# Attention: PE issues the next unit's first group of scores ahead of the router's rank matmuls and the V projection

## The chip, the cores and the metric

The kernel runs as one program on one core of one Trainium2 chip. The metric is the device time in microseconds of that core, from start to end of the program; smaller is better. The engines are PE (matrix multiplications), DVE (vector work), ACT (activation functions), POOL (general work, here also indirect DMAs) and SP (it only issues DMAs). Each has its own list of instructions, and they wait for each other through semaphores.

## The reference

The input is 64 sequences of 64 tokens with 128 channels and a context of the same shape. Four gated blocks follow each other: cross-attention, a top-2 mixture of 8 experts, a second kind of cross-attention, and a second mixture.

```python
x = x + tanh(g_xattn[0]) * L0_xattn(layernorm(x), ctx, ctx)
x = x + tanh(g_ffn[0])   * L0_ffn(layernorm(x))     # router, top 2 of 8 experts
x = x + tanh(g_xattn[1]) * L1_xattn(layernorm(x), ctx)
x = x + tanh(g_ffn[1])   * L1_ffn(layernorm(x))
```

The change lies in the first block. There, with 16 heads of 8 channels:

```python
wq = (q @ wq_w.T + wq_b).reshape(b, t, H, DH)
wk = (k @ wk_w.T + wk_b).reshape(b, t, H, DH)
wv = (v @ wv_w.T + wv_b).reshape(b, t, H, DH)
scores = einsum('bthd,bshd->bhts', wq, wk) / sqrt(DH)
probs = softmax(scores, axis=-1)
attn = einsum('bhts,bshd->bthd', probs, wv).reshape(b, t, d)
return attn @ wo_w.T + wo_b
```

The router of the second block (the logits, the two best experts, and where in the list of its expert each token goes) is worked out on the side, in the same loop as the attention.

## The kernel before

The tokens are 32 chunks of 128. A **unit** is two chunks (256 tokens, four sequences), and attention has 16 of them (`UA`). Each engine runs its own copy of a software pipeline, `it_a(u, s)`, whose order within a turn is written out by hand; turns go from -3 to 15, those from 3 to 10 in a hardware loop of two turns a pass. PE's turn `u` works on several units at once, one line of the code for each:

- `a_s(u + 1, g)`: scores of the next unit, four groups g of four heads, on `QT` and `Kb` (both are parts of the tensor `QK`), into bank 0 or 1 (L1572). Its first group waits for `a_qks`.
- `a_pt(u, g)`: transposes of the exponentials `Pr` of this unit (L1542). `a_pv(u, g)`: their product with V (L1590).
- `a_v(u)`: the V projection of this unit into bank 5 (L1555). It waits for `a_nrm`, since bank 5 holds the attention result of unit u - 1 until DVE has read it.
- `a_xt(u + 2)`, `a_qk(u + 2)`: transposes of the normalised tokens `xn` and the Q and K projections (L1562, L1563) of the unit after the next.
- `a_at(u - 1)`, `a_y(u - 1)`: the output projection of the unit before.
- `r_x(u - 2)`, `r_lg(u - 2)`, `r_rank(u - 3)`: the router. `r_rank` is five small bf16 matmuls (L1626 to L1630) on `chosen`; they count which place in its expert's list each token gets.

DVE's turn begins with `r_pos(u - 3)` (tile `pos`, L954), which waits for the ranks, then small router work up to `rowu` (L969), then the layer norm of unit u + 3 (tile `xn`, L838) and of the router's unit (tile `xr`), then `a_vs(u)` (tile `Vb`, L852), which copies V out of bank 5, and then for each group of unit u + 1 `a_max` (tile `mx`, L860) and `a_sub` (tile `Pr`, L864), which read the scores. It ends with the router's choice (`chosen`, L946), `a_rec` (L869) and `a_nrm` (tile `att`, L874).

ACT's turn copies PE's transposes out (`a_pts`, L590), takes the exponentials of `Pr` (L584), and between the second and the third of these scales and masks the Q and K of unit u + 2 in `a_qks` (four of L576 and four of L578), on which the first group of scores of that unit, in the next turn, depends.

POOL sends each router unit's tokens to their experts' lists with four indirect DMAs (L439) after `rowu`, and works out `pe`, a term of the weights (L432), which DVE's `den` (L922) needs. SP loads `cT`, the context of unit u + 2, once `a_v(u)` is done (L374).

Of the kernel before, what the change touches and what calls it, by code (L numbers as in the profile page):

```python
# [97 lines left out]
def flamingo(nc, x, ctx_tok, ctx_t, wq, wk, wv, wo, cols, rows, gates, consts, far,  # L98
             f0_wg, f0_w12, f0_w3, wqv, f1_wg, f1_w1, f1_w2, out):
    with ExitStack() as stack:  # L100
# [160 lines left out]
        def S(name):  # L261
            if name not in names:
                names[name] = sem(name)
            return names[name]
# [37 lines left out]
        def has(u, units=UA):  # L302

            return not isinstance(u, int) or 0 <= u < units
# [12 lines left out]
        def wait(eng, semaphore, value):  # L317

            if not isinstance(value, int) or value > 0:
                eng.wait_ge(semaphore, value)  # L320
# [1211 lines left out]
        def _(pe):  # L1532
# [7 lines left out]
            def transposes(done, dst, src, n):  # L1540
                for c in range(n):
                    last = nc.tensor.transpose(dst[:, P * c:P * (c + 1)], src(c), ident)  # L1542
                last.then_inc(S(done), 1)


            def a_xt(u, s):
                pe.wait_ge(S("a_ln"), u + 1)
                wait(pe, S("a_qks"), u)
                transposes("a_xt", bank[4], lambda c: xn[:, s, c, :], 2)

            def a_v(u, s):
                pe.wait_ge(S("a_nrm"), 1 + u)
                for b in range(4):
                    for e in range(2):
                        last = mm(bank[5][L * e:L * (e + 1), P * b:P * (b + 1)], cT[:, s, L * b:L * (b + 1)],  # L1555
                                  wv_eo[:, e, :], start=True, stop=True)
                last.then_inc(S("a_v"), 1)

            def a_qk(u, s):
                pe.wait_ge(S("a_xts"), u + 1)  # L1560
                pe.wait_ge(ld_cT[s], (u - s) * 8 + 16)
                mm(bank[4][:, 0:2 * P], wq_s[:], xT[:, 0, 0:2 * P], start=True, stop=True)  # L1562
                mm(bank[4][:, 2 * P:4 * P], wk_s[:], cT[:, s, 0:2 * P], start=True, stop=True).then_inc(S("a_qk"), 1)  # L1563

            def a_s(u, s, g):
                if g == 0:
                    pe.wait_ge(S("a_qks"), u + 1)
                wait(pe, S("a_sub"), u * 4 + (g - 1))
                for p in range(2):
                    for b in range(2):  # L1570
                        t = P * p + L * b
                        last = mm(bank[g % 2][L * b:L * (b + 1), 256 * p:256 * (p + 1)], QT[:, s, g, t:t + L],  # L1572
                                  Kb[:, s, :, t:t + L], start=True, stop=True)
                last.then_inc(S("a_s"), 1)

            def a_pt(u, s, g):
                pe.wait_ge(S("a_exp"), u * 4 + (g + 1))
                wait(pe, S("a_pts"), u * 4 + g)
                transposes("a_pt", bank[6 + g % 2], lambda c: Pr[:, s, g, P * c:P * (c + 1)], 4)

            def a_pv(u, s, g):
                pe.wait_ge(S("a_pts"), 1 + u * 4 + (g + 1))
                if g == 0:
                    pe.wait_ge(S("a_vs"), u + 1)
                for p in range(2):
                    for h in range(2):
                        for b in range(2):
                            m = (p * 8 + 2 * g + h) * 18
                            c = P * (2 * p + h) + L * b
                            last = mm(bank[5][L * b:L * (b + 1), m:m + 18], PT[:, g, c:c + L],  # L1590
                                      Vb[:, s, 2 * p + b, 2 * g + h, :], start=True, stop=True)
                if g == NG - 1:
                    last.then_inc(S("a_pv"), 1)

            def a_at(u):
                pe.wait_ge(S("a_nrm"), 1 + u + 1)
                pe.wait_ge(S("a_x"), 1 + u)
                transposes("a_at", bank[2], lambda c: att[:, D * c:D * (c + 1)], 2)

            def a_y(u):  # L1600
                pe.wait_ge(S("a_ats"), u + 1)
                mm(bank[2][:, 2 * P:4 * P], onb[:], rbias[:, 0:1, :].to_broadcast([P, 2, D]), start=True, stop=False, skip_group_check=True)
                for c in range(2):
                    last = mm(bank[2][:, P * (2 + c):P * (3 + c)], attT[:, P * c:P * (c + 1)], wo_s[:],
                              start=False, stop=True, skip_group_check=True)
                last.then_inc(S("a_y"), 1)
# [4 lines left out]
            def r_x(w, s):  # L1611
                pe.wait_ge(S("r_ln"), w + 1)
                pe.wait_ge(S("r_run"), w + 1)
                transposes("r_xt", bank[3], lambda c: xr[:, s, c, :], 2)

            def r_lg(w):
                pe.wait_ge(S("r_xts"), w + 1)
                for c in range(2):
                    last = mm(bank[3][:, 2 * P + E * c:2 * P + E * (c + 1)], xT[:, 1, P * c:P * (c + 1)], f0g_s[:], start=True, stop=True)
                last.then_inc(S("lgp"), 1)  # L1620

            def r_rank(w):

                pe.wait_ge(S("r_m"), w + 1)
                of = [bank[3][:, RK + E * c:RK + E * (c + 1)] for c in range(3)]
                mm(of[0], upb[:], chosen[:, 0, :], start=True, stop=True)  # L1626
                mm(of[1], onb[:], chosen[:, 0, :], start=True, stop=False)
                mm(of[1], upb[:], chosen[:, 1, :], start=False, stop=True)
                mm(of[2], onb[:], chosen[:, 0, :], start=True, stop=False)
                mm(of[2], onb[:], chosen[:, 1, :], start=False, stop=True).then_inc(S("r_rank"), 1)  # L1630

            def t_row(h):

                n = NW if h == 0 else NB - NW
                pe.wait_ge(S("t_col"), h + 1)
                mm(bank[3][0:1, TB:TB + NBH], first_row[:, h:h + 1], cst[:, C_ID + h * NBH:C_ID + (h + 1) * NBH], start=True, stop=True)
                for k in range(2):
                    w = C_BD + k * NB + h * NW
                    last = mm(bank[3][0:1, TB + NBH + n * k:TB + NBH + n * (k + 1)], en[:, h:h + 1], cst[:, w:w + n], start=True, stop=True)
                last.then_inc(S("t_row"), 1)  # L1640
# [4 lines left out]
            def it_a(u, s):  # L1645
                if has(u):
                    a_pt(u, s, 0)
                    a_pt(u, s, 1)
                if isinstance(u, int) and u == UT + 1:
                    pe.wait_ge(S("table"), 1)  # L1650
                if has(u - 3):
                    r_rank(u - 3)
                if has(u):
                    a_v(u, s)
                if has(u + 1):
                    a_s(u + 1, 1 - s, 0)
                if has(u - 1):
                    a_at(u - 1)
                if has(u + 2):
                    a_xt(u + 2, s)  # L1660
                if has(u + 1):
                    a_s(u + 1, 1 - s, 1)
                if has(u - 2):
                    r_x(u - 2, s)
                if has(u):
                    a_pt(u, s, 2)
                if has(u + 1):
                    a_s(u + 1, 1 - s, 2)
                if has(u + 2):
                    a_qk(u + 2, s)  # L1670
                if has(u):
                    a_pt(u, s, 3)
                if has(u - 1):
                    a_y(u - 1)
                if has(u - 2):
                    r_lg(u - 2)
                if has(u + 1):
                    a_s(u + 1, 1 - s, 3)
                if has(u):
                    a_pv(u, s, 0)  # L1680
                    a_pv(u, s, 1)
                    a_pv(u, s, 2)
                    a_pv(u, s, 3)
                if isinstance(u, int) and u == UT:
                    pe.wait_ge(S("lgs"), u - 1)
                    t_row(0)

            pipelined(pe, it_a, -3, 3, UT, UA)


# [312 lines left out]
```

## Time and profile before

| | us |
|---|---|
| median of 3 runs | 578.22 |
| lowest, highest | 575.12, 578.43 |
| the profiled execution's own time | 575.86 |
| its span, first to last instruction | 574.2 |
| PE busy, DVE busy, ACT busy, POOL busy | 503.0, 415.4, 316.8, 234.2 |

The rows of the next section come from that one profiled execution; their times count from the start of its span. 1.7 us of its time lie outside the span. The attention pipeline takes the part from about 20 to 232 us, and the steady turns with the router in them begin at about 67 us. Of the whole chain of work that ended last, 48% is PE, 20% DVE, 16% time in which the engine waited for nothing that the profile shows, 8% POOL and 4% ACT.

### The profile page before, as it was taken

What the parts mean: (1) busy time and instruction counts of PE and PEld (TensorE: products, weight loads), DVE (VectorE), ACT (ScalarE), POOL (GpSimd) and SP (SyncE); (2) the same over time, 40 slices, a digit from 0 to 9 for tenths busy, and PEclk for the clock granted to TensorE, in tenths of its full rate; (3) what the DMA queues carried; (4) which work ended last, traced back from release to release, by engine and by line L of the source; (5) the groups of instructions that cost most, each with busy time, mean ns of one, the idle gap of its engine ahead of it and who ended that gap; (6) DMA issues with size and microseconds to landing.
All of it is one profiled execution on the core that took longest, in us unless ns stands there. A gap on an engine that the chain in (4) does not pass through costs nothing.

```text
span 574.2 us, 14728 instructions
## 1 busy us (share of the span) xinstructions
PE 503.0 (88%) x4438; PEld 407.4 (71%) x4439; DVE 415.4 (72%) x1690; ACT 316.8 (55%) x777; POOL 234.2 (41%) x328
## 2 busy tenths in 40 slices
PE   0599999999988989878999999987989987997997
PEld 0267776777767667666778777866879975877897
DVE  4687888898989788556765567663777995575883
ACT  1378866677777764344555554554553555443453
POOL 2510255554454645445000545520566763022330
PEclk9999999999999999889999999996997999798999
DMA  8503011100000211135554334320010112000011
GB/s 246 241 10 85 23 36 33 32 27 27 27 27 29 67 47 32 48 107 170 163 165 121 107 107 110 93 66 15 23 28 12 50 43 61 6 1 0 2 39 37
DMA packets 48126, 36.80 MB, mean 64 GB/s; under 512 B 6466, under 2 KB 43970, under 8 KB 47812
## 3 DMA queue, kind: packets, MB, share of 16 engines
q1 hardware_dynamic: 31332, 21.13, 12.2%
q0 software_dynamic: 4640, 9.45, 5.7%
q10 hardware_dynamic: 12096, 5.51, 3.4%
q8 instruction: 28, 0.46, 0.4%
q14 instruction: 30, 0.25, 0.1%
HBM read 22.44 MB, written 13.63 MB: 63 GB/s over the span
## 4 chain that ended last, share of the span: by engine, by line
PE 48%; DVE 20%; issue 16%; POOL 8%; ACT 4%; another core or an unknown queue 2%; POOLq 1%; DVEq 1%; DMA 0%
PE bank L1542 10%; PE bank L1739 6%; PE bank L1837 5%; PE bank L1723 4%; POOL sent L439 4%; PE bank L1917 3%; PE bank L1725 3%; PE bank L1724 3%; PE bank L1572 3%; PE bank L1825 2%; DVE xn L838 2%; DVE mx L860 1%; DVE hgg L1415 1%; PE bank L1814 1%
## 5 line engine op out<-in xcount | busy, mean ns | idle before, releaser
L455 POOL DMA_INDIRECT yg<-done,gidx x64 | 63.8, 997 | 54.7 <-PE bank L1542 20.8
L439 POOL DMA_INDIRECT sent<-xr,rowu x64 | 62.9, 983 | 51.1 <-DVE rowu L969 36.4
L1572 PE MATMUL bank<-QK 128*64 128x256 f32 x512 | 70.6, 397 | 9.2 <-ACT QK L578 5.4
L424 POOL TENSOR_TENSOR ve<-mv,half 128x4 f32<-128x4 f32 (+1 forms) x40 | 10.3, 258 | 124.7 <-DVE mv L827 124.6
L1158 DVE TENSOR_TENSOR act<-sil,bank 128x256 f32<-128x256 f32 x80 | 33.6, 420 | 33.9 <-ACT sil L640 23.9
L590 ACT ACTIVATE PT<-bank 128x512 f32<-128x512 f32 x64 | 36.4, 602 | 36.2 <-PE bank L1542 35.9
L860 DVE TENSOR_REDUCE mx<-bank 128x8 f32<-128x512 f32 x64 | 43.7, 682 | 14.0 <-remote 9.4
L1739 PE MATMUL bank<-f0w_s,aT 128*128 x320 | 50.6, 281 | 3.6 <-DVE yb L1164 3.2
L1572 PEld LDWEIGHTS bank<-QK 128*64 128x64 f32 x512 | 32.3, 139 | 28.1 <-ACT QK L578 6.8
L640 ACT ACTIVATE sil<-bank 128x256 f32<-128x256 f32 x80 | 30.7, 384 | 37.5 <-PE bank L1725 33.3
L1739 PEld LDWEIGHTS bank<-f0w_s,aT 128*128 128x128 f32 x320 | 42.4, 193 | 5.7 <-issue 5.1
L864 DVE TENSOR_TENSOR Pr<-bank,mx 128x512 f32<-128x512 f32 x64 | 43.8, 684 | 1.2
L739 ACT ACTIVATE hg<-bank 128x512 f32<-128x512 f32 x32 | 19.2, 600 | 42.2 <-PE bank L1906 35.7
L635 ACT ACTIVATE xbh<-bank 128x128 fp32r<-128x128 f32 x80 | 22.2, 278 | 34.9 <-PE bank L1542 22.1
L1723 PE MATMUL bank<-f0w_h,xbh 128*128 x80 | 39.3, 491 | 0.7 <-issue 0.4
L584 ACT ACTIVATE Pr<-Pr 128x512 f32<-128x512 f32 x64 | 36.8, 629 | 5.4 <-DVE Pr L864 5.4
L427 POOL TENSOR_TENSOR ln<-ve,half 128x4 f32<-128x4 f32 (+3 forms) x40 | 37.1, 926 | 0.0
L1542 PE MATMUL bank<-cst,Pr 128*128 128x128 f32 x256 | 36.7, 277 | 0.0
L1590 PEld LDWEIGHTS bank<-Vb,PT 128*64 128x64 f32 x1024 | 33.0, 138 | 4.2 <-issue 2.0
L1917 PE MATMUL bank<-f1w_s,PT 128*128 128x128 f32 x256 | 33.8, 276 | 1.3 <-ACT PT L744 1.3
L1590 PE MATMUL bank<-Vb,PT 128*64 128x18 f32 x1024 | 32.6, 210 | 1.8 <-issue 1.8
L838 DVE TENSOR_SCALAR xn<-xs,ln 128x128 f32<-128x128 f32 (+1 forms) x96 | 31.6, 387 | 3.3 <-POOL ln L427 1.7
(220 smaller groups left out, 1341.9 us busy)
## 6 DMA issues: line engine op xcount, KB each, us to landing
xb<-sent SPq DMA_DIRECT2D x80, 64.0 KB
done<-yb ACTq DMA_DIRECT2D x80, 64.0 KB
xs<-x_dram SPq DMA_DIRECT2D x4, 512.0 KB, 7.1
cT<-ctx_t_dram SPq DMA_DIRECT2D x16, 128.0 KB
f0w_s<-f_w_dram SPq DMA_DIRECT2D x1, 2048.0 KB, 10.2
Pr<-ctx_t_dram SPq DMA_DIRECT2D x8, 256.0 KB
QK<-ctx_tok_dram SPq DMA_DIRECT2D x8, 256.0 KB
out_dram<-xs SPq DMA_DIRECT2D x8, 256.0 KB
```

The costliest lines, as they stand in the source:

```text
L427: nc.gpsimd.tensor_tensor(ln[:, bass.ds(u * n, n), 1], ve[:, h, 0:n], half[:, 2:3].to_broadcast([P, n]), ALU.pow).then_inc(S(f"ln{k}"), 1)
L439: nc.gpsimd.indirect_dma_start(sent, bass.IndirectOffsetOnAxis(ap=rowu[:, s, 2 * k + c:2 * k + c + 1], axis=0), xr[:, s, c, :], None).then ...
L455: nc.gpsimd.indirect_dma_start(yg[:, s, j, :], None, done[u // (U4 // HALVES)], bass.IndirectOffsetOnAxis(ap=gidx[:, s, j:j + 1], axis=0)) ...
L838: last = nc.vector.tensor_scalar(dst[:, c, :], xs[:, u * n + c, :], ln[:, u * n + c, 0:1], ln[:, u * n + c, 1:2], ALU.subtract, ALU.mult)
L860: nc.vector.tensor_reduce(mx[:, g, :], scores(g), AX, ALU.max).then_inc(S("a_max"), 1)
L864: nc.vector.tensor_tensor(Pr[:, s, g, :].rearrange("p (m k) -> p m k", k=L), scores(g), mx[:, g, :].unsqueeze(2).to_broadcast([P, 8, L]), ...
L1542: last = nc.tensor.transpose(dst[:, P * c:P * (c + 1)], src(c), ident)
L1572: last = mm(bank[g % 2][L * b:L * (b + 1), 256 * p:256 * (p + 1)], QT[:, s, g, t:t + L], Kb[:, s, :, t:t + L], start=True, stop=True)
L1590: last = mm(bank[5][L * b:L * (b + 1), m:m + 18], PT[:, g, c:c + L], Vb[:, s, 2 * p + b, 2 * g + h, :], start=True, stop=True)
L1723: mm(bank[1 - k][:], xbh[:, 1 - k, :], high, start=True, stop=False)
L1739: last_mm = mm(bank[2][:, 0:D], aT[:, 1 - k, j, :], f0w3_s[:, bass.ds(e, 1), j, :].rearrange("p e n -> p (e n)"), start=j == 0, stop=j == 1)
L1917: last = mm(bank[(6, 0)[k % 2]][:, 0:D], hT[:, k % 2, P * c:P * (c + 1)], f1w2_s[:, c, :], start=c == 0, stop=c == 3)
```

## The change

In PE's `it_a`, the first group of scores of the next unit, `a_s(u + 1, 1 - s, 0)`, is issued directly behind the transposes of groups 0 and 1 of this unit. Before, it came behind the router's ranks and the V projection. No other engine's list changes, and no wait is added or taken away.

```diff
                 if has(u):
                     a_pt(u, s, 0)
                     a_pt(u, s, 1)
+                if has(u + 1):
+                    a_s(u + 1, 1 - s, 0)
                 if isinstance(u, int) and u == UT + 1:
                     pe.wait_ge(S("table"), 1)
                 if has(u - 3):
                     r_rank(u - 3)
                 if has(u):
                     a_v(u, s)
-                if has(u + 1):
-                    a_s(u + 1, 1 - s, 0)
                 if has(u - 1):
                     a_at(u - 1)
```

PE's list at the head of a turn in the hardware loop, with what each instruction waits for, before; the last row of transposes is followed by the ranks, V and the scores:

```order
L1542 MATMUL bank<-cst,Pr 128x128 x3
L1624 REGISTER_ALU
L1626 MATMUL bank<-chosen,upb 128x8 [waits r_m]
L1627 MATMUL bank<-chosen,onb 128x8
L1628 MATMUL bank<-chosen,upb 128x8
L1629 MATMUL bank<-chosen,onb 128x8
L1630 MATMUL bank<-chosen,onb 128x8
L1552 REGISTER_ALU
L1555 MATMUL bank<-wv_eo,cT 64x128 [waits a_nrm]
L1555 MATMUL bank<-wv_eo,cT 64x128 x7
L1567 REGISTER_ALU
L320 ISA [waits a_qks]
```

The next row there is the first of the four matmuls of the scores (L1572). The same place in the changed kernel:

```order
L1542 MATMUL bank<-cst,Pr 128x128 x3
L1567 REGISTER_ALU
L320 ISA [waits a_qks]
L1572 MATMUL bank<-QK 64x256 [waits a_sub]
L1572 MATMUL bank<-QK 64x256 x3
L1624 REGISTER_ALU
L1626 MATMUL bank<-chosen,upb 128x8 [waits r_m]
L1627 MATMUL bank<-chosen,onb 128x8
L1628 MATMUL bank<-chosen,upb 128x8
L1629 MATMUL bank<-chosen,onb 128x8
L1630 MATMUL bank<-chosen,onb 128x8
L1555 MATMUL bank<-wv_eo,cT 64x128 [waits a_nrm]
```

The wait for `a_qks` and the four matmuls behind it now stand ahead of the wait for `r_m` (the tile `chosen`) and that for `a_nrm`.

The same move in turn 0, where there is no router yet, as PE's list stands before:

```order
L1542 MATMUL bank<-cst,Pr 128x128 [waits a_pts,a_exp]
L1542 MATMUL bank<-cst,Pr 128x128 x3
L1555 MATMUL bank<-wv_eo,cT 64x128 [waits a_nrm]
L1555 MATMUL bank<-wv_eo,cT 64x128 x7
L1572 MATMUL bank<-QK 64x256 [waits a_sub,a_qks]
L1572 MATMUL bank<-QK 64x256 x3
```

and as it stands in the changed kernel:

```order
L1542 MATMUL bank<-cst,Pr 128x128 [waits a_pts,a_exp]
L1542 MATMUL bank<-cst,Pr 128x128 x3
L1572 MATMUL bank<-QK 64x256 [waits a_sub,a_qks]
L1572 MATMUL bank<-QK 64x256 x3
L1555 MATMUL bank<-wv_eo,cT 64x128 [waits a_nrm]
L1555 MATMUL bank<-wv_eo,cT 64x128 x7
```

Here the scores have moved past the V projection alone.

## Rows read from the trace of the kernel before

**Rows 1.** Busy time of each engine, 100 to 140 us

```profile
core 0: us, PE busy (x) PEld busy (x) DVE busy (x) ACT busy (x) POOL busy (x), PEclk, DMA share, GB/s
...
100.00:140.00 40.00, 36.84 (x461) 28.24 (x462) 36.30 (x131) 28.35 (x60) 21.52 (x28) 1.00 0.10 31
```

**Rows 2.** Timeline of DVE in turn 6: start, length, what, idle before

```profile
107.37 0.16 DVE L954 TENSOR_TENSOR pos<-bank,run 128x16 f32<-128x16 f32 x1
...
108.66 0.66 DVE L838 TENSOR_SCALAR xn<-xs,ln 128x128 f32 x2 [0.16 <-issue]
...
109.79 0.68 DVE L852 COPY Vb<-bank 128x512 f32<-128x512 f32 x1
...
111.11 0.69 DVE L864 TENSOR_TENSOR Pr<-bank,mx 128x512 f32<-128x512 f32 x1
...
120.42 0.17 DVE L954 TENSOR_TENSOR pos<-bank,run 128x16 f32<-128x16 f32 x1 [0.18 <-issue]
```

**Rows 3.** Timeline of PE in turn 6

```profile
105.16 1.09 PE L1542 MATMUL bank<-cst,Pr 128*128 128x128 f32 x8
...
106.78 0.18 PE L1626 MATMUL bank<-chosen,upb 128*128 128x8 bf16 x1 [0.53 <-DVE chosen L946]
...
107.50 1.09 PE L1555 MATMUL bank<-wv_eo,cT 128*64 128x128 f32 x16 [0.44 <-DVE att L874]
...
108.43 1.03 PE L1572 MATMUL bank<-QK 128*64 128x256 f32 x8
...
111.86 1.08 PE L1572 MATMUL bank<-QK 128*64 128x256 f32 x8
```

**Rows 4.** Timeline of ACT around turn 6

```profile
105.17 1.93 ACT L578 ACTIVATE QK<-bank,bkm,cst 128x256 f32<-128x256 f32 x4
...
114.88 0.60 ACT L590 ACTIVATE PT<-bank 128x512 f32<-128x512 f32 x1 [2.38 <-PE bank L1542]
...
118.32 1.93 ACT L578 ACTIVATE QK<-bank,bkm,cst 128x256 f32<-128x256 f32 x4
```

**Rows 5.** Timeline of turn 1, in the start-up

```profile
44.03 1.93 ACT L578 ACTIVATE QK<-bank,bkm,cst 128x256 f32<-128x256 f32 x4
...
45.50 0.69 DVE L852 COPY Vb<-bank 128x512 f32<-128x512 f32 x1 [0.72 <-PE bank L1555]
...
46.02 1.08 PE L1572 MATMUL bank<-QK 128*64 128x256 f32 x8 [0.57 <-ACT QK L578]
...
47.04 0.44 PE L1542 MATMUL bank<-cst,att 128*128 128x128 f32 x2
...
49.23 1.08 PE L1572 MATMUL bank<-QK 128*64 128x256 f32 x8
```

**Rows 6.** Timelines of turn 3, of turn 12 and of turn 14

```profile
66.74 1.93 ACT L578 ACTIVATE QK<-bank,bkm,cst 128x256 f32<-128x256 f32 x4
...
68.27 0.17 DVE L954 TENSOR_TENSOR pos<-bank,run 128x16 f32<-128x16 f32 x1
...
185.72 0.18 PE L1626 MATMUL bank<-chosen,upb 128*128 128x8 bf16 x1 [0.95 <-DVE table L1047]
...
186.04 0.17 DVE L954 TENSOR_TENSOR pos<-bank,run 128x16 f32<-128x16 f32 x1 [0.38 <-PE bank L1630]
...
210.51 1.94 ACT L578 ACTIVATE QK<-bank,bkm,cst 128x256 f32<-128x256 f32 x4
...
212.48 0.16 DVE L954 TENSOR_TENSOR pos<-bank,run 128x16 f32<-128x16 f32 x1
```

**Rows 7.** Timeline of DVE in turn 13

```profile
201.15 0.17 DVE L922 TENSOR_SCALAR den<-pe 128x2 f32<-128x2 f32 x1 [2.23 <-POOL pe L432]
```

**Rows 8.** Timeline of SP's queue, then the busy times of one later stretch

```profile
34.16 11.65 SPq L374 DMA_DIRECT2D cT<-ctx_t_dram  x2
...
36.00:36.50 0.50, 0.50 (x6) 0.32 (x6) 0.37 (x1) 0.50 (x2) 0.50 (x1) 1.00 0.00 0
```

**Rows 9.** Busy times behind the last turns, columns as in rows 1

```profile
230.00:232.00 2.00, 0.86 (x24) 0.93 (x24) 0.00 (x0) 0.00 (x0) 1.91 (x5) 1.00 0.10 33
...
234.00:236.00 2.00, 2.00 (x8) 1.54 (x8) 0.39 (x3) 1.97 (x5) 0.00 (x0) 0.50 0.18 53
```

## The prediction

> **What bounds the kernel now.** The move touches only the attention part, some 205 of the 574 us, so I read that part alone. First the busy time by stretch [rows 1]: in 40 us of the steady part PE works 36.84 us, DVE 36.30 and ACT 28.35. Two engines are nearly full, so the order of their waits decides, and the timeline has to be read unit by unit (a unit is one turn of `it_a`, two chunks of tokens). I number the turns by the `u` of PE's `it_a`; the example is turn 6, at 105 to 118 us.
>
> DVE is the engine without slack [rows 2]: from `pos` (L954) of turn 6 at 107.37 to `pos` of turn 7 at 120.42 it goes through its list almost without a gap, 13.05 us. `pos` needs the rank matmuls, and they came in time. PE [rows 3] transposes groups 0 and 1 until 105.16 + 1.09 = 106.25, waits 0.53 for `chosen`, does the ranks at 106.78, waits 0.44 for `att`, does V at 107.50, and then at 108.43 the first group of scores of the next unit, S0. S0 needs QT and Kb of that unit, which ACT writes last with L578. ACT [rows 4] ends that at 105.17 + 1.93 = 107.10. So today this wait is covered: S0 comes 1.33 us after its operands. Where the new order puts S0, right behind the transposes, they are missing for another 0.85 us, and the ranks, V and all that DVE does with them stand behind it.
>
> **The change, part by part.** No instruction goes or comes apart from register work; S0 (four matmuls in 8 passes, 1.02 us from its start to that of the next thing, 46.02 to 47.04 in [rows 5]) moves ahead of the ranks and V. S0's other wait, `a_sub` of group 2 of the unit before, is over long before. What changes is the time of each of three things.
>
> 1. S0 itself starts as soon as ACT is done. In the start-up, where the old order already waited there, S0 starts at 46.02 after L578's end at 44.03 + 1.93 = 45.96 [rows 5], so 0.06 us later. An earlier S0 is worth nothing to DVE, because `mx` of group 0 stands behind `pos`, `xn`, `xr` and `Vb` in DVE's list.
>
> 2. The ranks come 1.01 to 1.02 us behind S0's start, and `pos` 0.32 us behind the ranks' start: that is the gap in the one turn where DVE really waited for them, 185.72 to 186.04 [rows 6]. With q for the end of L578, `pos` can start at q + 0.06 + 1.01 + 0.32 = q + 1.39 at the earliest. Against the old `pos`: turn 3, the first, q = 68.67 and `pos` 68.27, so 1.79 later; turn 6, 107.10 and 107.37, 1.12 later; turn 14, the last, 212.45 and 212.48, 1.36 later [rows 2, 4, 6]. There are eleven such turns (3 to 12 and 14). The ten from 3 to 12 add up to 12.4 us (they lie between 0.9 and 1.8), and turn 14 adds 1.36.
>
> 3. These add up, they don't merely shift once, because the delay closes a circle. `pos` to the end of the first `Pr` (L864) is pure DVE work, 107.37 to 111.11 + 0.69 = 111.80. The third group of scores waits for just that and starts at 111.86 [rows 3]. Behind it PE does QK and the transposes of group 3, on which ACT waits 2.38 us (114.88), then two exponentials and L576, L578: the next q is 118.32 + 1.93 = 120.25 [rows 4]. So `pos` to the next q is 12.88 us, all of it a chain, and the next `pos` comes 1.39 after it: a turn takes 12.88 + 1.39 = 14.27 us where it took about 13.0. PE itself would allow it: V ends at about q + 2.3, `xn` is ready at `pos` + 1.95, and the third group could go at q + 5.6, while `Pr` lets it go at q + 5.9. DVE's list gets about 1.2 us of idle time ahead of `pos` in each turn.
>
> 4. Turns 0 to 2 have no ranks; there V moves behind S0, and `Vb`, then `mx` of group 0, wait for V. In turn 1 V now starts at 46.02 + 1.02 = 47.04, takes 1.09 [rows 3], and `Vb` follows at 48.17. From `Vb` to `Pr`, with `mx` between, is 109.79 to 111.11 = 1.32 us [rows 2], so `Pr` runs from 49.49 to 50.18, and the third group, which was at 49.23, starts at 50.24: 1.0 us [rows 5]. Turn 0 worked out the same way gives 1.2, turn 2 0.9. Together 3.2 us.
>
> 5. Turn 13 adds nothing: DVE waits there 2.23 us for POOL's `pe` until 201.15 [rows 7], which is 15.1 us behind `pos` of turn 12. The new `pos` of turn 13 comes 12.8 + 1.39 = 14.2 behind it and still waits for POOL. Turn 12's table wait (0.95 us of PE, rows 6 at 185.72) now has part of S0 beneath it, which is in the 1.07 that this turn adds.
>
> 6. V's end also releases SP's next load of cT (L374). V moves back against its own turn, but QK, which wants the load, moves back as far: 4.3 us between them in turn 6 before, 4.5 after. In turn 0 it falls to about 3.1. A load issued at 34.16 has left no DMA traffic from 36.00 on [rows 8], so 1.84 us: it stays covered, and would cost up to 1 us once if it weren't. POOL's sends hang on `rowu`, a fixed step behind `pos`, and move along; the wait of DVE behind POOL's weight split lies after the first `Pr`, off the new chain.
>
> Sum: 3.2 + 12.4 + 1.4 = 17.0 us. Everything behind attention starts that much later and is unchanged. The profiled execution took 575.86 us, which lies between the runs' lowest (575.12) and their median 578.22; the sum gives 592.9 from it and 595.2 from the median. I say **594 us**.
>
> **Bounds.** Low: the start-up costs nothing and each of eleven turns only turn 6's 1.12: 12.3 us, 588. High: each of eleven turns costs the 1.79 of the first, and three 1.2 of turn 0: 23.3 us, or 601 from the median. What I can't read is whether the gap of 0.32 from ranks to `pos` holds behind S0, some 0.1 either way a turn, which takes the low end to 587.
>
> **Rivals.** (a) *The wait is paid once*: ACT catches up after the first delay and finds itself ahead, so later turns wait only for `pos` as before. Then it is 3.2 + 1.8 = 5 us, 581. For it: ACT is idle 30% of the time. Against it: the idle time lies ahead of L590 and waits for PE [rows 4], inside the circle of step 3. 5%.
> (b) *Faster, the gap is filled*: S0 goes into PE's 0.53 + 0.44 us of idle time around the ranks [rows 3], PE's list gets 0.97 us shorter in twelve turns, and if PE and not DVE sets the pace, that is 11.6 us off: 564. It decides at one point: L578 must end before the transposes of group 1 do. It ends 0.85 us after in turn 6, and even S0 at 106.25 would put the ranks at 107.26, 0.5 later than they were. 3%.
> (c) *The clock falls too*: PE's idle time becomes one piece of 0.9 to 1.9 us ahead of S0 and another of some 0.7 ahead of `xn`. The only place near here with a lower clock is 234 to 236 us, granted 0.50, the 1.2 GHz level, after PE had worked only 0.86 of the 2 us from 230 on [rows 9]. A steady turn keeps PE at work for nearly 12 of 14.3 us, and it stood at 1.00 in [rows 1]. If it fell in each of eleven turns for three microseconds of PE work at half speed, that is 1.5 us each, 610. 5%. The Trainium skill, "TensorE: Matmul & The Clock Gate", Part 1, says the same of direction: an idle stretch drops the clock to half and sustained work brings it back. By it the chance hangs on short gaps alone, and rows 5 show a wait of 0.57 us after which S0 still took 1.08.
> (d) *The ranks get past the waiting S0*, and nothing changes, 578. No row shows matmuls out of order; turn 12's ranks waited 0.95 for the table with V behind them [rows 6]. I give this nothing. The Trainium skill, same page, Part 2, "Step-by-step", has only weight loads pulled ahead on PE while matmuls keep the program's order; by it this case falls away as well.
>
> **How the numbers follow.** The forecast has 87%, (a) 5, (b) 3, (c) 5. About 1% (6 us) is what a measurement of this kernel can tell from no change; (a) is under it, the forecast and (c) over it: slower 0.92, same 0.05, faster 0.03. The range 586 to 602 holds the forecast's bounds with 1 us on either side and leaves (a), (b) and (c) outside.
>
> **What would show it.** In the new trace S0 should carry an idle time with ACT's L578 as releaser in every turn, the ranks about 1.0 us after it; DVE should sit idle 1.0 to 1.3 us ahead of L954, released by PE's L1630, eleven times, and ahead of `Vb` in turns 1 and 2; turns 3 to 11 should come every 14.2 to 14.3 us; everything from 235 us on should look the same, 17 us later. I am wrong if DVE's idle time ahead of L954 is there but the turns are no longer, or if L578 ends before PE gets to S0.

## The result, and the profile after

| | before | changed |
|---|---|---|
| median, us (4 runs each) | 578.33 | 596.21 |
| lowest to highest, us | 575.12 to 579.10 | 591.91 to 602.44 |
| profiled execution, us | 575.86 | 594.04 |
| its span, us | 574.2 | 592.4 |

The changed kernel takes 1.0278 times the kernel before, with a 95% interval of 1.022 to 1.0336: 16.1 us slower, 12.7 to 19.4. The forecast was 17.0 us more. One of the four changed runs, 602.44 us, was slow at a lower granted clock (0.949, the others 0.954 to 0.968) and is in the median but not in the ratio, so the medians lie 17.9 us apart and the ratio gives 16.1.

The timeline of PE and DVE in turn 6 of the changed kernel, with ACT's last step, answers to [rows 2 to 4]:

```profile
116.80 1.93 ACT L578 ACTIVATE QK<-bank,bkm,cst 128x256 f32<-128x256 f32 x4
116.81 1.09 PE L1542 MATMUL bank<-cst,Pr 128*128 128x128 f32 x8
...
118.67 0.42 DVE L874 TENSOR_TENSOR att<-bank,rec 128x256 f32<-128x256 f32 x1
...
118.86 1.08 PE L1572 MATMUL bank<-QK 128*64 128x256 f32 x8 [0.96 <-ACT QK L578]
...
119.88 0.18 PE L1626 MATMUL bank<-chosen,upb 128*128 128x8 bf16 x1
...
120.09 1.09 PE L1555 MATMUL bank<-wv_eo,cT 128*64 128x128 f32 x16
...
120.20 0.17 DVE L954 TENSOR_TENSOR pos<-bank,run 128x16 f32<-128x16 f32 x1 [1.10 <-PE bank L1630]
...
123.86 0.69 DVE L864 TENSOR_TENSOR Pr<-bank,mx 128x512 f32<-128x512 f32 x1
...
124.61 1.08 PE L1572 MATMUL bank<-QK 128*64 128x256 f32 x8 [1.02 <-DVE Pr L864]
```

PE is done with the transposes at 117.90 and then stands for 0.96 us. ACT ends L578 at 118.73, and the scores (S0) start 0.13 later, the ranks 1.02 behind them, `pos` 0.32 behind the ranks. DVE had `att` behind it at 119.09 and sat idle for 1.10 us. The third group starts 0.06 after the first `Pr`. That is the chain of the forecast, link by link. Its period, again from the timeline of DVE, the first and the last of the nine turns that follow each other without table work:

```profile
77.19 0.17 DVE L954 TENSOR_TENSOR pos<-bank,run 128x16 f32<-128x16 f32 x1 [1.79 <-PE bank L1630]
...
191.45 0.17 DVE L954 TENSOR_TENSOR pos<-bank,run 128x16 f32<-128x16 f32 x1 [1.33 <-PE bank L1630]
```

114.26 us for eight turns is 14.28 a turn, against 104.74 / 8 = 13.09 for the same turns before (68.27 to 173.01). In the stretch of [rows 1] all three engines lose, since the same work is spread over more time:

```profile
core 0: us, PE busy (x) PEld busy (x) DVE busy (x) ACT busy (x) POOL busy (x), PEclk, DMA share, GB/s
...
100.00:140.00 40.00, 33.30 (x437) 24.84 (x433) 33.71 (x125) 27.51 (x59) 18.75 (x26) 1.00 0.08 26
```

And the waits of the steady turns, 76 to 192 us (who waits for whom, total, times, longest), show the two new ones, DVE behind the ranks and PE behind ACT, of which the kernel before had neither in the same turns:

```profile
DVE pos L954 <- PE bank L1630: 13.8, 9, 1.9
...
PE bank L1572 <- ACT QK L578: 9.3, 9, 1.2
```

### The profile page after: what moved, and what is told of

It reads as the page before. It is cut to its first block, busy times and chain, and to the rows that moved or that the text cites. A ratio compares the mean times of both kernels' runs of the same rounds, so it can differ in the third digit from the quotient of the medians.

```text
span 592.4 us, 14724 instructions
## 1 busy us (share of the span) xinstructions
PE 506.0 (85%) x4438; PEld 407.7 (69%) x4439; DVE 420.6 (71%) x1690; ACT 317.6 (54%) x777; POOL 233.8 (39%) x328
## 4 chain that ended last, share of the span: by engine, by line
PE 57%; DVE 15%; issue 12%; ACT 11%; POOL 2%; DVEq 1%; DMA 0%; another core or an unknown queue 0%; POOLq 0%; ACTq 0%
PE bank L1542 12%; PE bank L1572 8%; PE bank L1739 5%; PE bank L1837 5%; PE bank L1723 3%; ACT QK L578 3%; PE bank L1917 3%; ACT QK L576 3%; PE bank L1725 3%; PE bank L1724 3%; ACT Pr L584 2%; PE bank L1555 2%; DVE xn L838 2%; PE bank L1562 2%; PE bank L1590 2%
## 5 line engine op out<-in xcount | busy, mean ns | idle before, releaser
L1572 PE MATMUL bank<-QK 128*64 128x256 f32 x512 | 74.2, 413 | 32.3 <-ACT QK L578 20.8
L1572 PEld LDWEIGHTS bank<-QK 128*64 128x64 f32 x512 | 32.8, 143 | 55.4 <-issue 19.9
L590 ACT ACTIVATE PT<-bank 128x512 f32<-128x512 f32 x64 | 36.4, 601 | 47.8 <-PE bank L1542 47.1
```

## The experiments

The eight ran on two chips, e1, e2, e4 and e5 on one and e3, e6, e7 and e8 on the other, each group with its own runs of the kernel before (medians 568.18 and 568.28 us). The kernel before took 578.33 us in the runs above, so I take them to be from a third chip, some 2% slower; which chip they ran on is not known. I therefore compare ratios, and turns with turns of these two chips. A turn here is the mean distance of `pos` over the eight turns from turn 3 to turn 11. In the old order it is 12.86 us in e1, 12.88 in e3 and 12.86 in e7, so the two chips agree. Microseconds below are the ratio times 568.3.

| | edit | ratio to before, 95% | us |
|---|---|---|---|
| e1 | scores ahead of V only | 1.0081 (1.0046 to 1.0116) | +4.6 |
| e2 | the move from turn 3 on | 1.0168 (1.0106 to 1.023) | +9.5 |
| e3 | the move in turns -1 to 2 | 1.0065 (1.0028 to 1.0102) | +3.7 |
| e4 | old order, POOL's split later | 0.9921 (0.9885 to 0.9957) | -4.5 |
| e5 | new order, POOL's split later | 1.0267 (1.0215 to 1.032) | +15.2 |
| e6 | new order, L578 shorter | 1.0144 (1.0122 to 1.0167) | +8.2 |
| e7 | old order, L578 shorter | 1.0023 (0.9996 to 1.0049) | +1.3 |
| e8 | e4 with the output projection earlier | 0.9934 (0.991 to 0.9958) | -3.8 |

### e1: half of the move

```diff
                 if has(u - 3):
                     r_rank(u - 3)
-                if has(u):
-                    a_v(u, s)
                 if has(u + 1):
                     a_s(u + 1, 1 - s, 0)
+                if has(u):
+                    a_v(u, s)
```

> Half of the move: the scores go ahead of the V projection, but stay behind the ranks. My theory (the ranks' place is what costs; the circle is end of L578, scores, ranks, pos, first Pr, third group, L578): pos of DVE is on time again, V ends at q + 2.3, which is before Vb's old start in the steady turns, so turns 3 to 11 come every 13.0 us as before. Left are 3.2 us in turns 0 to 2 (4.6 where the clock falls in turn 1), 0.2 in turn 12, 0.9 in turn 14: 4 to 6 us over the kernel before, 583. Rival (it is V's delay or the wait of PE's whole list that costs, wherever the ranks stand): nearly all of the 17 us stays, 594.

Measured: 4.6 us (2.6 to 6.6), inside the 4 to 6 of my theory; the rival is out. The timeline of turn 4 shows the point:

```profile
85.24 0.17 PE L1626 MATMUL bank<-chosen,upb 128*128 128x8 bf16 x1
...
85.80 0.16 DVE L954 TENSOR_TENSOR pos<-bank,run 128x16 f32<-128x16 f32 x1
...
86.17 1.08 PE L1572 MATMUL bank<-QK 128*64 128x256 f32 x8 [0.66 <-ACT QK L578]
...
87.08 1.05 PE L1555 MATMUL bank<-wv_eo,cT 128*64 128x128 f32 x16
...
88.23 0.68 DVE L852 COPY Vb<-bank 128x512 f32<-128x512 f32 x1
```

PE waits 0.66 us for L578 here too, and it costs this turn nothing: `pos` goes on time, V ends at 88.13 and `Vb`, at its old distance of 2.43 from `pos`, doesn't wait. The turns (12.57, 12.71, 13.10, 12.68 and so on) are those of the old order. So it is not PE's wait that costs but that the ranks are queued behind it.

### e2 and e3: the move split by place

One flag in `it_a` decides in which turns the scores go first; e2 has `u >= 3` (and the hardware loop), e3 `u < 3`.

```diff
+                early = not isinstance(u, int) or u >= 3
                 if has(u):
                     a_pt(u, s, 0)
                     a_pt(u, s, 1)
+                if early and has(u + 1):
+                    a_s(u + 1, 1 - s, 0)
...
-                if has(u + 1):
+                if not early and has(u + 1):
                     a_s(u + 1, 1 - s, 0)
```

> The whole move, but only from turn 3 on; turns -1 to 2 keep the old order. My theory: 12.4 + 1.4 = 13.8 us, a turn takes 14.28 us in turns 3 to 11, 592. Rival (the wait is paid once and ACT is then ahead): 1.8 us, 580.

> The whole move, but only in turns -1 to 2; from turn 3 on the order of the kernel before. My theory: 3.2 us by the sum of the prediction, up to 4.6 where PE's wait of 1.6 us in turn 1 drops the clock, as the changed kernel's trace shows it: ratio 1.006 to 1.008. Turns 3 to 11 as in the kernel before. Rival (a late start-up upsets the steady turns as well): ratio over 1.014.

Measured: e2 9.5 us (6.0 to 13.1), under the 13.8 forecast, whose value lies just outside the interval; the rival's 1.8 is far out. Its turns take 13.97 us on average against 12.88 in e3, so 1.09 each here, where the kernels above gave 1.19. DVE's timelines, first e2 and then e3:

```profile
72.05 0.17 DVE L954 TENSOR_TENSOR pos<-bank,run 128x16 f32<-128x16 f32 x1 [1.78 <-PE bank L1630]
...
183.80 0.17 DVE L954 TENSOR_TENSOR pos<-bank,run 128x16 f32<-128x16 f32 x1 [0.94 <-PE bank L1630]
```

```profile
73.20 0.17 DVE L954 TENSOR_TENSOR pos<-bank,run 128x16 f32<-128x16 f32 x1
...
176.22 0.17 DVE L954 TENSOR_TENSOR pos<-bank,run 128x16 f32<-128x16 f32 x1
```

In e2 `pos` of turn 3 to `pos` of turn 14 takes 152.99 us against 142.00 in e3, 11.0 more, and `pos` of turn 3 itself waits 1.78 for the ranks; together that is 12.8 of the 13.8 forecast. The mechanism stands; the price of a turn was a little lower on this chip. e3 gives 3.7 us (1.6 to 5.8), between the 3.2 of the sum and 4.6. Together the halves make 13.2 us, against 15.2 for the whole move in e5, inside the intervals.

### e4 and e5: take DVE's stall away, in either order

In the kernel before, DVE loses some 1.5 us in each of turns 3 to 10 around L930, at the time when POOL splits an expert's weights (L464). In turn 5 it is L930 itself that takes 1.98 us in place of 0.22; in turn 6 L930 is short and DVE then idles for 1.50:

```profile
100.08 1.98 DVE L930 TENSOR_SCALAR kept_w<-den,tg 128x2 f32 x1
...
100.74 1.29 POOL L464 TENSOR_TENSOR f0w_s<-f0w_s,f0w_h  x1
...
113.04 0.22 DVE L930 TENSOR_SCALAR kept_w<-den,tg 128x2 f32 x1
...
113.92 1.28 POOL L464 TENSOR_TENSOR f0w_s<-f0w_s,f0w_h  x1
...
114.77 0.69 DVE L860 TENSOR_REDUCE mx<-bank 128x8 f32<-128x512 f32 x1 [1.50 <-remote]
```

The edit makes POOL wait until DVE is past both kept weights.

```diff
             def w12_low(e):
                 pool.wait_ge(S("w12_h"), e + 1)
+                pool.wait_ge(S("w"), e * 2 + 2)
```

> The order of the kernel before, and POOL's split of the expert weights (L464) in turns 3 to 10 waits until DVE has written both kept weights of that turn (L930, L934), so that it runs 2 to 3 us later, beside the second half of DVE's turn. My theory: in the old order DVE's list sets the pace, and the 1.5 us that DVE loses at L930 or ahead of the third mx to POOL's split are on the path; they go in eight turns, and PE's own list (about 11.8 us of work and gaps) becomes the next bound: a turn of 11.8 to 12.3, 6 to 10 us faster, 570. Rival (the stall has another cause than the split, or moves to another DVE instruction beside it): no change.

> The changed kernel with the same later split on POOL. My theory: there the pace is set by the circle over ACT's L578, and DVE's stall lies behind the first and second Pr, off that circle; it goes, and DVE's idle time ahead of pos grows by as much, from 1.1 or 1.8 to 2.6 or more. The turn stays at 14.28 us and the time at that of the changed kernel, 594 to 596. Rival (DVE's list still sets the pace in the new order): 8 to 12 us under the changed kernel, 586.

This pair is the sharpest test of which engine sets the pace. The added line moves the numbers of the lines behind it by one. DVE in e5, timeline from the kept weight of turn 6 to `pos` of turn 7:

```profile
121.03 0.22 DVE L931 TENSOR_SCALAR kept_w<-den,tg 128x2 f32 x1
121.16 0.68 DVE L861 TENSOR_REDUCE mx<-bank 128x8 f32<-128x512 f32 x1
...
127.04 0.42 DVE L875 TENSOR_TENSOR att<-bank,rec 128x256 f32<-128x256 f32 x1
129.31 0.17 DVE L955 TENSOR_TENSOR pos<-bank,run 128x16 f32<-128x16 f32 x1 [1.84 <-PE bank L1631]
```

The stall is gone (0.22 us, and the next instruction follows at once) in both kernels. In the old order the turn falls from 12.86 (e1, on the same chip) to 12.29 us, eight times, and the kernel gains 4.5 us (2.4 to 6.5). In the new order the turn is 13.97 us as in e2, and the time is that of the changed kernel (1.0267, 1.0278): all of what DVE saves, it waits longer for the ranks, 1.82 to 1.84 us in turns 4 to 10, where e2 has 1.43 to 1.50 or 0.91 to 0.93. The changed order has taken DVE off the path.

Of the 6 to 10 us expected of e4 only 4.5 came, and of the 1.5 us of stall only 0.57 a turn. DVE there waits 0.59 us a turn for the output projection (L1605, 4.7 us in the eight turns), and I took that for the reason; e8 below shows that it isn't. The traces show a better one. In e3, DVE's fourth `mx` starts 1.48 to 2.08 us behind the start of the fourth group of scores in turns 3 to 10, because DVE gets there late. In e4 it is 1.13 or 1.14 in every one of them, which is the group's own 1.08 and 0.05: without the stall DVE waits there for PE. Turn 6 of e4, PE and DVE:

```profile
114.64 1.08 PE L1573 MATMUL bank<-QK 128*64 128x256 f32 x8
...
115.77 0.69 DVE L861 TENSOR_REDUCE mx<-bank 128x8 f32<-128x512 f32 x1
```

The trace of e4 also has something that the argument above leaves out. In turn 13, after two waits of 1.08 and 1.05 us, the granted clock fell to 0.50, and the turn took 15.87 us where e3 took 14.23:

```profile
199.69 1.62 PE L1573 MATMUL bank<-QK 128*64 128x256 f32 x8 [1.05 <-DVE Pr L865]
```

```profile
201.00:202.00 1.00, 1.00 (x4) 0.68 (x3) 0.74 (x3) 0.00 (x0) 0.69 (x2) 0.50 0.28 78
```

The second block is the busy times from 201 to 202 us, columns as in [rows 1], with a granted clock of 0.50. So in that one execution 1.6 us of the 4.5 from the eight turns were lost again. Whether the others had the same fall no trace shows.

### e6 and e7: make ACT's last step shorter

Two of L578 write two heads of Kb each, with the bias and mask of the first. The second head of each pair gets the wrong mask, so the result is not the reference's; the instructions on the other engines stay the same.

```diff
-                for j in range(HG):
-                    last = nc.scalar.activation(Kb[:, s, j, :], bank[4][:, 2 * P:4 * P], ACT.Identity,
+                for j in range(0, HG, 2):
+                    last = nc.scalar.activation(Kb[:, s, j:j + 2, :], bank[4][:, 2 * P:4 * P].unsqueeze(1).to_broadcast([P, 2, 2 * P]), ACT.Identity,
                                                 bias=bkm[:, j:j + 1], scale=cst[:, C_KM + j:C_KM + j + 1])
```

> The changed kernel with ACT's last step shortened: two of L578 write two heads of Kb each in place of four that write one, about 1.15 us in place of 1.93. The two heads of a pair get the first one's bias and mask, so the scores aren't the reference's. My theory (the end of L578 is what PE, then DVE wait for): PE's wait ahead of the scores and DVE's idle time ahead of pos both shrink by 0.8, the turn from about 13.98 (14.28 on the first chip) to 13.2, eleven times, and the start-up gains 2: 10 to 11 us under the changed kernel, ratio to the kernel before 1.008 to 1.01. Rival (the four score matmuls ahead of the ranks cost by their own length, whatever they wait for): 3 us under the changed kernel at most, ratio 1.022.

> The same shortened L578 (the two heads of a pair share one bias and mask) in the order of the kernel before, as the control. My theory: in the old order the scores come over 1 us after L578's end in the steady turns, so nothing changes there; turns 0 to 2, where PE waits 0.3 to 0.9 us for L578, gain 2 us in all: ratio 0.996. Rival (ACT's length is on the path in the old order too): ratio 0.985 or less.

```profile
84.30 1.45 ACT L578 ACTIVATE QK<-bank,bkm,cst 128x512 f32<-128x512 f32 x2
...
85.88 1.08 PE L1572 MATMUL bank<-QK 128*64 128x256 f32 x8 [0.28 <-ACT QK L578]
```

L578 fell from 1.93 to 1.45 us (timeline of turn 4 in e6), 0.48 and not the 0.8 I had expected. The turn fell from 13.97 in e2 and e5 to 13.49, by 0.48: one to one. PE's wait went from about 0.77 to 0.28, DVE's ahead of `pos` by as much, and the time by 7 us against e5, which measured the same as the changed kernel (14 turns with this chain times 0.48 is 6.7). The rival, that the scores cost by their own length whatever they wait for, allowed 3 us. The control e7 shows no gain in the old order, 1.0023. I had expected 2 us there from the start-up turns; they don't show in the interval of 0.9996 to 1.0049. In the traces 0.5 of the 2 us came: from the end of L578 ahead of turn 0 to that ahead of turn 3 it is 33.20 us in e7 (36.51 to 69.71) and 33.72 in e4 (36.59 to 70.31), whose order is the same there.

### e8: one step further from e4

```diff
-                if has(u):
-                    a_pt(u, s, 3)
                 if has(u - 1):
                     a_y(u - 1)
+                if has(u):
+                    a_pt(u, s, 3)
```

> The old order with POOL's later split, and on PE the output projection (a_y) ahead of the transposes of group 3. In the run with the later split alone DVE waited 0.59 us a turn for that projection. My theory: that wait goes and the transposes come 0.5 us later, which ACT and L578 pass on; L578 then ends just when PE gets to the scores. A turn of 11.9 to 12.1 in place of 12.26, and 1.2 us less in turns 13 and 14: ratio 0.985 to 0.989. Rival (PE's list or the third group's chain over ACT is the bound by now): ratio 0.992 as without this edit, or up to 0.996 through the later transposes.

The rival has it: 0.9934 against 0.9921 for e4, the same within the intervals, and a turn of 12.32 us against 12.29 (the 12.26 above is e4's mean over six of the turns). DVE no longer waits for the projection, but 0.23 us for the router's logits (L1620) right behind it, and then again for the fourth group. Turn 6 of e8:

```profile
113.88 1.08 PE L1573 MATMUL bank<-QK 128*64 128x256 f32 x8
...
115.01 0.69 DVE L861 TENSOR_REDUCE mx<-bank 128x8 f32<-128x512 f32 x1
```

Again 1.13 us behind the start of the fourth group, and PE, with its list in another order but as long, gets from V to that group in 7.83 us in both kernels. From V of turn 6 to V of turn 7 both take 12.10 us. In turn 13 the clock fell here too (15.76 us). The best version is e4, which beats both kernels: the old order with POOL's split of the weights put behind DVE's kept weights.

## Why the prediction was right

**What bounds the kernel.** DVE's list set the pace before: e4 shows it, where taking the stall out of DVE alone shortened the turn, and e5 shows that the new order took DVE off the path. But its lead was small: of 1.5 us of stall 0.57 a turn were gained before PE's fourth group of scores became the next wait.

**Step 1, S0 starts with L578's end.** Right, with 0.13 us in the hardware loop in place of 0.06 (118.73 to 118.86). e1 adds that an S0 that waits is harmless in the steady turns as long as only V stands behind it.

**Step 2, `pos` at q + 1.39.** It came at 120.20 against 118.73, q + 1.47: 1.02 and 0.32 as forecast, and the 0.07 of step 1. Turns 3 to 12 together cost 11.9 us in the two kernels above (`pos` of turn 12 is 18.90 late, L578's end ahead of turn 3 was 7.04 late), forecast 12.4.

**Step 3, the circle.** 14.28 us a turn, forecast 14.27. Its two parts were off by 0.06 and 0.07, and the misses cancel: `pos` to the end of L578 took 12.82 on average in turns 3 to 10 for the forecast's 12.88, and from there to `pos` 1.46 for its 1.39. That it is a circle and not a shift is shown by e2, whose turns are all about 1.1 us longer than the old ones, and by e6, where 0.48 us off ACT came off every turn.

**Step 4, the start-up.** 3.2 us forecast, e3 measured 3.7. In the changed kernel's own trace turn 0 costs 1.09 (L578's ends 37.60 and 49.71 against 34.94 and 45.96) and turn 2 0.87, near the 1.2 and 0.9. Turn 1 costs 2.4 in place of 1.0, because there the clock fell, the part of rival (c) that came true here: the forecast had no term for a single fall. In e3, where it didn't fall, the same turn took 12.12 us (49.16 to 61.28) against 11.24 in e4. PE's timeline:

```profile
49.77 1.97 PE L1572 MATMUL bank<-QK 128*64 128x256 f32 x8 [1.59 <-ACT QK L578]
51.53 1.76 PE L1555 MATMUL bank<-wv_eo,cT 128*64 128x128 f32 x16
```

The busy times by stretch, with the columns of the stretch above, have for it:

```profile
50.00:52.00 2.00, 2.00 (x14) 1.24 (x14) 0.00 (x0) 1.72 (x4) 0.00 (x0) 0.50 0.04 8
```

A granted clock of 0.50 is the 1.2 GHz level, after 1.59 us without work. It fell once more behind a wait of 2.08 us for L578 in turn 14: 1.00 up to 232 us and 0.50 from 234 to 236. In the steady turns, with waits of 0.96 to 1.2, it stood at 1.00 as I had argued.

**Step 5, turn 13 adds nothing.** Right: `den` comes 15.11 us behind `pos` of turn 12, as before to the hundredth, released by POOL:

```profile
204.94 0.17 DVE L954 TENSOR_TENSOR pos<-bank,run 128x16 f32<-128x16 f32 x1 [0.83 <-PE bank L1630]
...
220.05 0.17 DVE L922 TENSOR_SCALAR den<-pe 128x2 f32<-128x2 f32 x1 [0.80 <-POOL pe L432]
```

Turn 14 then cost more than its 1.36: from there to the next `pos` it was 14.07 us against 11.33, 2.74 more. The forecast's 1.36 is one half of it. The other 1.38 lies between the third group (223.36) and ACT's L590 (227.36), 4.00 us where the same turn took 2.62 before (204.46 to 207.08). PE's rows between the two keep their distances, and its transposes of group 3 end at 225.94; in the kernel before L590 started 0.04 behind them, here 1.42:

```profile
225.34 0.60 PE L1542 MATMUL bank<-cst,Pr 128*128 128x128 f32 x4
...
227.36 0.60 ACT L590 ACTIVATE PT<-bank 128x512 f32<-128x512 f32 x1 [4.26 <-PE bank L1542]
```

So it was ACT that came late; why stays open. It isn't a fixed price: on the other chips the same stretch takes 12.68 us in e5 and 10.84 in e3, 1.84 more, which is what the forecast's reckoning gives there, since `pos` of turn 14 in e3 comes 0.45 ahead of the end of L578 (215.20, 215.65), and 0.45 + 1.39 = 1.84.

**The sum.** 17.0 us forecast, 16.1 measured (12.7 to 19.4). The two profiled executions differ by 18.2 us, and not all of that is the change: ahead of turn 0, in code that is the same, the changed kernel's was 2.66 us late already, since PE's matmuls ran at the slow level until about 36 us and not 29, and behind attention it made up 3.6 (from the ranks at 232.50 and 254.29 to the ends of the spans, 341.7 and 338.1 us). Between, the start-up took 4.4 of it (3.2 forecast), turns 3 to 12 took 11.9 (12.4) and turn 14 took 2.7 (1.4). So the mechanism and the price of a turn were right, but that the sum comes within 0.9 us of the measured ratio is partly luck: the fall of the clock in turn 1 and ACT's late start in turn 14 were not in it, and neither were the 3.6 us made up behind attention, whose cause I haven't followed.

**Rivals.** (a), paid once, fell with e2. (b), the filled gap, fell at the point named: L578 ended 0.83 us after the transposes. (c) came true in turns 1 and 14 of one trace, not in the steady turns. (d) fell: the ranks never passed S0.

## What to carry to other kernels

Before work is moved ahead in a list, look up when its operands come in the trace, not whether the engine has idle time there: this S0 fitted into 0.97 us of idle time, but its operands were 0.85 us late, and behind it stood the five tiny matmuls that DVE's whole turn begins with. A wait is free with only uncritical work behind it (the steady turns of e1) and costs in full, every turn, with critical work behind it (e2, e6). And the engine that sets the pace is found by giving it time back: the same edit to POOL was worth 4.5 us in one order and nothing in the other. That a wait is gone (DVE's for the output projection in e8) doesn't mean that time is gained, if another one ends just behind it.

## What the runs showed of the hardware

- The clock fell after a short gap in some kernels and not in others. In turn 1 PE waited 1.59 us for L578 in four kernels' traces; S0 then took 1.97 us in the changed kernel's and 1.08 in those of e1, e3 and e5. In turn 13 PE waited 1.03 to 1.08 us and soon after 1.04 or 1.05 in e3, e4, e6, e7 and e8; the granted clock then fell to 0.50 in e4, e6 and e8 and stood at 1.00 in e3 and e7. It cost e4 1.64 us (15.87 against 14.23 from `pos` to `pos` in e3).
- The granted clock can read 1.00 while matmuls run at half speed: S0 of turn -1, at 23 to 26 us, took 1.97 to 1.98 us for its 8 passes in every trace, at a granted clock of 1.00, against 1.08 in the steady turns.
- A DVE instruction on 2 elements a partition (L930) took 1.98 us beside POOL's weight split in place of 0.22, though it had started 0.66 us before it (100.08, 100.74); in other turns the 1.5 us came as idle time behind it, and in e3 as 1.45 us in L934. With the split moved away all three went, eight turns out of eight. The Trainium skill, "Advanced Engine Details and Errata", section "VectorE Performance Modes", has GpSimd and DVE's two-port instructions block each other at a shared SBUF port. e4 and e5 agree in that the stall goes with the overlap; that it is the port no run here shows.
